# Attention scores from two float32r products per tile, made on chip, with a merged front

## Chip, core and metric

The kernel runs on one core of one Trainium2 chip. The time is the device time of one execution in microseconds, from the first instruction to the last, with a little around it. Three runs of the kernel before gave 888.09, 890.4 and 890.46 us; their median is 890.4 us.

## What is computed

One decoder layer with post-normalisation, for 4 sequences of 512 tokens with 256 features, all in float32. Only the first line is touched by the change:

```python
x = _layernorm(x + _L0_attn_ref(x, w_q, w_k, w_v, w_o))
#   q, k, v = x @ w_q.T, x @ w_k.T, x @ w_v.T            16 heads of 16
#   weights = softmax(einsum('bqhd,bkhd->bhqk', q, k) * 16**-0.5)
#   out     = einsum('bhqk,bkhd->bqhd', weights, v);  out @ w_o.T
x = _layernorm(x + _L0_xattn_ref(x, ctx, ctx, ...))      # 64 keys per sequence
x = _layernorm(x + _L0_ffn_ref(x, router_w, w1, w2))     # 8 experts, the best 2 per token
```

The scores go through an exponential, so they are needed nearly as exactly as float32 gives them.

## The kernel before

**Work and names.** There are NB = 4 sequences (batches) b. A *unit* u is four heads of one sequence (HG = 4 heads, NU = 4 units a batch, 16 units in all). A *tile* is 128 x 512 scores of one head; a unit has 16 tiles of scores with queries on the partitions, of which only the row maximum is wanted (*maximum tiles*, `max_half`, L1233), and 16 tiles with keys on the partitions, whose exponentials are kept (*exponential tiles*, `exp_tile`, L1288). The value product (`pv`, L1297) multiplies four exponential tiles, one of each head, with the values; its four heads lie on four groups of 32 columns of TensorE (PE), and a column of ones gives the sum of the softmax. The maximum of a query is subtracted inside the product of the exponential tile, as extra rows of the contraction.

**Exactness.** A score tile is one bfloat16 product. q and k are each split into three bfloat16 parts, and six products of parts (`Q_PART`, `K_PART`) are laid under each other as 96 rows of contraction; three rows more carry the parts of the maximum. To have these rows on the right partitions, the parts go to DRAM and come back.

**The front.** For each batch PE projects q, k and v in float32 (`project`, L1254, L1257), ScalarE (ACT) and VectorE (DVE) make the three parts (L732, L878, L735, L363), and the queue of SyncE (SP) writes them to DRAM (L387) and reads them back as stacks `qst` and `kst` in 12 DMAs (L393), `make_stacks`. The parts of batch b + 1 can't be overwritten before those of b are stored. Maximum tiles of the first two units run between the projections of batches 2 and 3. The three rows of maxima of unit 0 are written to `qst` by DMAs (`max_rows`, L400) that stand on SP's queue between the stacks.

**The units.** PE's order in `unit` (L1304) is written by hand: exponential tiles of unit u alternate with maximum tiles of unit u + 2, value products stand two tiles behind the fourth exponential tile, and the maxima of unit u + 1 are turned from partitions to rows once (`max_turn`, L1240). DVE takes the row maxima (`row_max`, L890), copies the turned maxima (`max_T`, L898) and the finished output of a unit to `oT` (L955). ACT takes the exponentials (L745). GpSimd (POOL) splits the maxima (`max_parts`) and lays out the values (`v_unit`). Four banks of PSUM hold maximum tiles, three hold exponential tiles, one the value products.

**Behind it.** From L1356 on, output projection, cross-attention, router and experts follow. The change leaves their code as it is, but for places in memory. Late weights and the residual x are loaded in the last batch of units.

The unit loop of PE, where its order is made:

```python
            for kt in range(QT):
                for h in range(HG):
                    exp_tile(u, HG * kt + h)
                    ...
                    if has_m and h < HALVES[kt]:
                        max_half(u + 2, half_at, j + 2)
                        half_at += 1
                    if h == 2 and kt > 0:
                        pv(u, b, kt - 1, j)
```

## Time and profile before

| | us |
|---|---|
| median of three runs | 890.4 |
| the profiled execution, as timed | 889.74 |
| its span (first to last instruction) | 888.0 |
| front: projections, stacks, holes, until the units run without a stop | 0 to 141.06 |
| the rest of the units of self-attention | 141.06 to 324.39 |
| everything behind | 324.39 to 888.0 |

The page gives the busy time of each engine over the whole span. Its 40 slices show where an engine is busy; a slice is 22.2 us. Since the stages have different limits, the busy time is read stage by stage (windows), and what an engine waits for is read from the chain of waits and from the instructions in order of time. A matmul's duration in the trace contains its latency; what it costs in a stream is the time from its start to the next start.

### The profile page before, as it was taken

The page shows a single profiled execution, that of the slowest core. Times are in us where ns is not written, and L with a number is a line of the kernel's source. Part 1 is how long each engine was busy: PE and PEld are TensorE (multiplying, and loading weights), DVE is VectorE, ACT ScalarE, POOL GpSimd, SP SyncE. Part 2 cuts the span into 40 slices and gives each one's busy share as a digit, 9 for nine tenths or more (in the row PEclk, how much of TensorE's full clock was granted, in tenths as well). Part 3 has the DMA queues.
Part 4 walks back from the last instruction along what each step waited for, and adds up shares of the span by engine and source line. Part 5 has one row for each costly group of instructions (what it writes and reads, how often), then busy time and mean ns, then how long its engine had stood idle before and what let it go on. Part 6 is the DMA issues. An engine that isn't in the chain of part 4 may idle for free.

```text
span 888.0 us, 13256 instructions
## 1 busy us (share of the span) xinstructions
PE 686.3 (77%) x4099; PEld 449.1 (51%) x4100; DVE 349.9 (39%) x750; ACT 285.8 (32%) x501; POOL 212.3 (24%) x265
## 2 busy tenths in 40 slices
PE   7572266999999986764677862099999999999980
PEld 3230111322222245541213652089999999999970
DVE  2252344888888546653443875000000000000004
ACT  3220133767666643332354211011111111111112
POOL 1020100111111122112111067213333333333322
PEclk9876786999999999886689995599999999999995
DMA  6999992000001430858713722356666566656615
GB/s 207 129 170 169 141 151 32 3 1 1 1 1 44 136 53 37 134 82 130 98 53 101 250 77 50 105 161 180 175 169 177 167 173 180 174 174 175 170 45 189
DMA packets 75777, 103.61 MB, mean 117 GB/s; under 512 B 15044, under 2 KB 60637, under 8 KB 75742
## 3 DMA queue, kind: packets, MB, share of 16 engines
q1 hardware_dynamic: 63006, 90.53, 45.0%
q0 software_dynamic: 8512, 8.44, 5.8%
q10 hardware_dynamic: 4224, 4.19, 1.7%
q8 instruction: 19, 0.31, 0.2%
q14 instruction: 16, 0.13, 0.1%
HBM read 82.95 MB, written 21.40 MB: 118 GB/s over the span
## 4 chain that ended last, share of the span: by engine, by line
PE 64%; DMA 14%; DVE 7%; SPq 5%; POOL 4%; issue 3%; ACT 2%; DVEq 0%; ACTq 0%; POOLq 0%
PE ps L1566 16%; PE ps L1577 15%; PE ps L1288 7%; DMA scrq<-parts 7%; PE ps L1297 7%; PE ps L1233 5%; SPq L393 3%; POOL metas L664 3%; DMA qst<-mT 3%; PE ps L1381 2%; PE ps L1454 2%; PE ps L1447 2%; DMA qst<-scr_q 1%; PE ps L1413 1%; DVE xr L993 1%
## 5 line engine op out<-in xcount | busy, mean ns | idle before, releaser
L890 DVE TENSOR_REDUCE nmx<-ps 128x1 f32<-128x512 f32 x256 | 160.4, 681 | 55.0 <-PE ps L1233 55.0
L745 ACT ACTIVATE probs<-ps 128x512 f32<-128x512 f32 x256 | 133.8, 606 | 93.7 <-PE ps L1288 93.6
L1566 PEld LDWEIGHTS ps<-xtT,w1c 128*128 128x128 f32 x1248 | 147.1, 194 | 4.3 <-issue 2.4
L1566 PE MATMUL ps<-xtT,w1c 128*128 128x128 f32 x1248 | 147.6, 277 | 1.8 <-ACT xtT L845 1.8
L1577 PE MATMUL ps<-wexp,hidT 128*128 x624 | 141.0, 379 | 0.0
L1198 DVE TENSOR_SCALAR yw<-ps,mt 128x256 f32<-128x256 f32 x39 | 18.9, 484 | 292.2 <-PE ps L1577 292.2
L1577 PEld LDWEIGHTS ps<-wexp,hidT 128*128 128x128 f32 x624 | 115.6, 190 | 14.2
L1288 PE MATMUL ps<-qst,kst 99*128 (+1 forms) x256 | 96.4, 396 | 33.9 <-DMA qst<-mT 31.8
L1233 PE MATMUL ps<-kst,qst 96*128 (+1 forms) x256 | 94.6, 396 | 33.6 <-DVE nmx L890 17.3
L851 ACT ACTIVATE hidT<-ps 128x1024 f32<-128x1024 f32 x39 | 40.0, 1024 | 229.8 <-PE ps L1566 229.8
L703 POOL DMA_INDIRECT acc<-yw,mt x39 | 61.7, 1582 | 172.0 <-DVE yw L1198 172.0
L1288 PEld LDWEIGHTS ps<-qst,kst 99*128 (+1 forms) x256 | 23.8, 99 | 120.3 <-issue 92.0
L1297 PE MATMUL ps<-probs,vu 128*32 128x512 f32 x512 | 68.2, 605 | 1.9 <-ACT probs L745 1.4
L1233 PEld LDWEIGHTS ps<-kst,qst 96*128 (+1 forms) x256 | 25.5, 100 | 66.0 <-issue 26.9
L808 ACT ACTIVATE probs<-ps 64x512 f32<-64x512 f32 x64 | 35.5, 587 | 42.9 <-PE ps L1447 42.8
L695 POOL DMA_INDIRECT xt<-x2d,mt x39 | 40.8, 1047 | 31.6 <-DMA mt<-metas 12.2
L532 POOL TENSOR_TENSOR m<-nmx,one 128x16 bf16<-128x16 f32 x16 | 3.5, 217 | 181.4 <-PE ps L1233 111.3
L1447 PE MATMUL ps<-qst,k2st 99*64 99x512 bf16 x64 | 27.1, 471 | 15.2 <-DMA qst<-mT 9.6
L664 POOL DMA_INDIRECT metas<-meta,slot x32 | 31.7, 990 | 22.4 <-DVE slot L1140 13.3
L1555 PE MATMUL ps<-identf,xt 128*128 128x128 f32 x78 | 15.2, 277 | 28.2 <-DMA xt<-x2d,mt 28.2
L878 DVE SCALAR_TENSOR_TENSOR tmp<-ps,parts 128x1024 f32<-128x1024 f32 x8 | 9.8, 1219 | 57.4 <-ACT parts L732 57.4
L1393 PE MATMUL ps<-identf,xr 128*128 128x128 f32 x64 | 14.1, 362 | 22.7 <-DVE xr L993 21.9
(162 smaller groups left out, 668.1 us busy)
## 6 DMA issues: line engine op xcount, KB each, us to landing
w1c<-in_w1T SPq DMA_DIRECT2D x39, 1024.0 KB
wexp<-in_w2T SPq DMA_DIRECT2D x8, 1024.0 KB, 5.5
qst<-scrq SPq DMA_DIRECT2D x24, 256.0 KB, 9.2
kst<-scrk SPq DMA_DIRECT2D x24, 256.0 KB, 19.7
qst<-scr_q SPq DMA_DIRECT2D x24, 256.0 KB, 8.8
scrq<-parts SPq DMA_DIRECT2D x4, 768.0 KB, 18.1
scrk<-parts SPq DMA_DIRECT2D x4, 768.0 KB, 18.6
scr_q<-parts SPq DMA_DIRECT2D x4, 768.0 KB, 3.4
```

What stands on the lines that cost most here:

```text
L664: pool.indirect_dma_start(metas, bass.IndirectOffsetOnAxis(slot[b % 2][:, k * QT + t:k * QT + t + 1], 0), meta[k][:, 2 * (QT * b + t):2 * ...
L695: pool.indirect_dma_start(xt[t % 2][:, :], None, x2d, bass.IndirectOffsetOnAxis(slot_meta(t, 0).bitcast(U32), 0), **checked()).then_inc(s_ ...
L703: pool.indirect_dma_start(acc, bass.IndirectOffsetOnAxis(slot_meta(t, 0).bitcast(U32), 0), yw[t % 2][:, :], None, **checked(), compute_op= ...
L745: act.activation(probs[n % 8][:, :], ps[:, 4 + n % 3, :], ACT.Exp).then_inc(s_exp, 1)
L851: act.activation(hidT[j % 2][:, :], bank(2 * (j % 2), 2), ACT.Gelu).then_inc(s_h, 1)
L890: dve.tensor_reduce(nmx[j % 2][:, k:k + 1], ps[:, slot, :], AX.X, ALU.max, negate=True).then_inc(s_mfree, 1)
L1233: pe.matmul(ps[:, tile_slot(j, k, isinstance(w, int) and w == 0), :], qst[0:ROWS, ds((w * HG + h) * S + qt * P, P)], kst[0:ROWS, ds((w * H ...
L1288: pe.matmul(ps[:, 4 + n % 3, :], kst[:, ds((u * HG + h) * S + kt * P, P)], qst[:, ds((u * HG + h) * S, S)], start=True, stop=True).then_in ...
L1297: mm = pe.matmul(ps[VW * h:VW * (h + 1), 7, :], vu[j % 2][:, (kt * HG + h) * VW:(kt * HG + h + 1) * VW], probs[(kt % 2) * HG + h][:, :], s ...
L1447: pe.matmul(ps[0:SC, 4 + h % 2, :], k2st[0:MROWS, ds((h * NB + b) * SC, SC)], qst[0:MROWS, ds((b * H + h) * S, S)], start=True, stop=True) ...
L1566: mm = pe.matmul(ps[:, 2 * (j % 2) + f // 4, f % 4 * P:(f % 4 + 1) * P], w1c[j % 2][:, k * FF + f * P:k * FF + (f + 1) * P], xtT[j % 2][:, ...
L1577: mm = pe.matmul(ps[:, 4 + j % 2, 0:D], hidT[j % 2][:, f * P:(f + 1) * P], wexp[:, ds(e * EW + f * D, D)], start=(f == 0), stop=(f == KF - 1))
```

## The change

**Scores.** The stacks, the three bfloat16 parts and the way through DRAM are gone. The weights of q and k are laid out with every head's 16 columns twice (`wqd`, `wkd`, by DVE for the first unit and POOL for the others), so that a projection of one unit (four heads) has 128 rows, 32 for each head, with q (or k) in them twice. From the projection in PSUM, ACT and DVE write four tiles of type float32r, a float32 of fewer mantissa bits: `qb` holds the high numbers of q, `qa` high and low numbers (the low ones negated), `ka` the high numbers of k, the second 16 rows with the sign turned, `kb` the low numbers of k, over whose second rows ones are laid. A score tile is then two products that add in one bank, each on the 32 rows of its head: `qa` with `ka`, and the first 16 rows of `qb` with `kb`. For exponential tiles the second product has two rows more, high and low number of the maximum against ones (`MAX_ROWS`). The four heads of a unit lie on four groups of 32 rows.

**Maxima.** They are turned as float32 without a split, DVE writes high and low numbers (`mT_hi`, `mT_lo`), and eight DMAs a unit put them in `qb`. Two DMAs a unit write the ones.

**Order.** A short front projects q0 and k0 of the first batch; 26 maximum tiles (`LEAD`) are taken ahead, with five more projections between. Then PE takes two exponential tiles, two maximum tiles, a value product after every second such step, and a projection of the same or the next batch at places of a table. Everything is unrolled. Maximum and exponential tiles have three banks each.

```diff
+LEAD = 26
+TURN_AT = 3
+HIGHS = 2 * HD
+MAX_ROWS = 2
+PROJECTIONS = ("q0", "k0", "q1", "k1", "v0", "q2", "k2", "v1", "q3", "k3")
...
+    PROLOGUE = {1: "q1", 4: "k1", 8: "v0", 12: "q2", 16: "k2"}
+    FIRST_BATCH_AT = {2: "v1", 6: "q3", 11: "k3"}
+    NEXT_BATCH_AT = [dict(zip(at, PROJECTIONS)) for at in
+                     ((15, 20, 25, 30, 35, 41, 46, 51, 57, 62), (3, 9, 17, 23, 29, 35, 41, 47, 53, 59))]
...
     @block.sync
-        def make_stacks(b):
...
+        def ones_rows(u):
+            sp.wait_ge(s_kb, u + 1)
+            for r in range(HD, HD + MAX_ROWS):
+                sp.dma_start(kb[u % (2 * NU)][r:P:HIGHS, :].bitcast(F32).rearrange("p (a t) -> p a t", a=HG),
+                             onesr[:, :].unsqueeze(1).to_broadcast([HG, HG, S // HG])).then_inc(s_one[u % NU], 16)
+        def max_rows(w):
+            sp.wait_ge(s_mfree, turn_slot(w) + 1)
+            for r, m in ((HD, mT_hi), (HD + 1, mT_lo)):
+                for i in range(HG):
+                    sp.dma_start(qb[w % (2 * NU)][HIGHS * i + r:HIGHS * i + r + 1, :].bitcast(F32).rearrange("p (a t) -> p a t", t=P),
+                                 m[w % 2][QT * i:QT * (i + 1), :].bitcast(F32)).then_inc(s_mrow[w % 2], 16)
...
     @block.scalar
+        def q_high(b, u, name):
+            act.wait_ge(s_proj, proj_number(b, name) + 1)
+            act.activation(qb[(NU * b + u) % (2 * NU)][:, :], ps[:, proj_bank(b, name), :], ACT.Copy).then_inc(s_qb, 1)
+        def k_high(b, u, name):
+            act.wait_ge(s_proj, proj_number(b, name) + 1)
+            act.activation(ka[(NU * b + u) % (2 * NU)][:, :], ps[:, proj_bank(b, name), :], ACT.Identity,
+                           scale=sign[:, 0:1]).then_inc(s_ka, 1)
...
+        for e in range(UNITS * TILES):
+            act.wait_ge(s_e, e + 1)
+            if e % HG == 0 and e >= 8:
+                act.wait_ge(s_pv, e // HG - 1)
+            act.activation(probs[e % 8][:, :], ps[:, 3 + e % 3, :], ACT.Exp).then_inc(s_exp, 1)
+            for b, name in projections_at(e):
+                evict(b, name)
...
     @block.vector
+        def q_both(b, u, name):
+            dve.wait_ge(s_qb, n + 1)
+            dve.scalar_tensor_tensor(out=qa[n % (2 * NU)][:, :], in0=ps[:, proj_bank(b, name), :], scalar=not_low[:, 0:1],
+                                     in1=qb[n % (2 * NU)][:, :], op0=ALU.mult, op1=ALU.add).then_inc(s_qa, 1)
+        def k_low(b, u, name):
+            dve.wait_ge(s_ka, n + 1)
+            dve.tensor_tensor(kb[n % (2 * NU)][:, :], ps[:, proj_bank(b, name), :], ka[n % (2 * NU)][:, :],
+                              ALU.subtract).then_inc(s_kb, 1)
...
+        for e in range(UNITS * TILES):
+            maxima(e + LEAD)
+            if e % TILES == 1 and e >= TILES:
+                o_out(e // TILES - 1)
+            for b, name in projections_at(e):
+                evict(b, name)
...
     @block.tensor
+        def max_tile(w, k):
...
+            pe.matmul(ps[:, n % 3, :], qa[u][both, qt * P:(qt + 1) * P], ka[u][both, :], start=True, stop=False)
+            pe.matmul(ps[:, n % 3, :], qb[u][highs, qt * P:(qt + 1) * P], kb[u][highs, :], start=False,
+                      stop=True).then_inc(s_mready, 1)
...
+        def exp_tile(e):
+            if e >= 3:
+                pe.wait_ge(s_exp, e - 2)
+            w, both, more = u % (2 * NU), slice(HIGHS * i, HIGHS * (i + 1)), slice(HIGHS * i, HIGHS * i + HD + MAX_ROWS)
+            pe.matmul(ps[:, 3 + e % 3, :], ka[w][both, kt * P:(kt + 1) * P], qa[w][both, :], start=True, stop=False)
+            pe.matmul(ps[:, 3 + e % 3, :], kb[w][more, kt * P:(kt + 1) * P], qb[w][more, :], start=False,
+                      stop=True).then_inc(s_e, 1)
...
+        for e in range(0, UNITS * TILES, 2):
+            for pair in range(2):
+                exp_tile(e + pair)
+            for pair in range(2):
+                maxima(e + LEAD + pair)
+            if e % HG == 0 and e >= HG:
+                pv(e // HG - 1)
+            for b, name in projections_at(e) + projections_at(e + 1):
+                project(b, name)
```

The order on PE, in the middle of a unit. Before (L1297 is the value product, L1288 an exponential tile, L1233 a maximum tile, L1240 the turn):

```order
L1297 MATMUL ps<-probs0_113,vu0_121 32x512 [waits probs_ready,v_unit_ready]
L1297 MATMUL ps<-probs1_114,vu0_121 32x512
L1297 MATMUL ps<-probs2_115,vu0_121 32x512
L1297 MATMUL ps<-probs3_116,vu0_121 32x512
...
L1288 ISA [waits probs_ready]
L1288 MATMUL ps<-qst_98,kst_99 128x512
...
L1233 ISA [waits max_scores_used]
L1233 MATMUL ps<-kst_99,qst_98 128x512
```

And after, in unit 6 of the changed kernel (L1292 and L1293 are the two products of an exponential tile, L1241 and L1242 those of a maximum tile, L1273 a projection, L1306 the value product):

```order
L1293 MATMUL ps<-qb6_116,kb6_132 128x512
L1241 MATMUL ps<-ka7_125,qa7_109 128x512 [waits max_scores_used]
L1242 MATMUL ps<-kb7_133,qb7_117 128x512
L1241 MATMUL ps<-ka7_125,qa7_109 128x512 [waits max_scores_used]
L1242 MATMUL ps<-kb7_133,qb7_117 128x512
L1273 MATMUL ps<-xTb2_139,wqd_153 128x512 [waits v_half_ready]
L1273 MATMUL ps<-xTb2_139,wqd_153 128x512
L1292 MATMUL ps<-qa6_108,ka6_124 128x512 [waits probs_ready]
L1293 MATMUL ps<-qb6_116,kb6_132 128x512
L1292 MATMUL ps<-qa6_108,ka6_124 128x512 [waits probs_ready]
...
L1306 MATMUL ps<-probs0_142,vu1_135 32x512 [waits probs_ready,o_ready]
```

Each tile has two products in a row where it had one, tiles go in pairs, and the projections of later batches stand between them.

The order on SP's queue at the start. Before, the maxima of unit 0 (L400) stand behind the stacks (L387, L393) of three batches:

```order
L387 DMA scrq<-parts_101 128x2x1536 [waits part3_ready]
L387 DMA scrk<-parts_102 128x2x1536 [waits part3_ready]
L393 DMA qst<-scrq 16x16x512 [waits q_parts_stored,stacks_loaded]
L393 DMA qst<-scrq 16x16x512 x5
L393 DMA kst<-scrk 16x16x512 [waits k_parts_stored]
L393 DMA kst<-scrk 16x16x512 x5
L400 DMA qst<-mT_96 1x16x128 [waits max_scores_used]
L400 DMA qst<-mT_96 1x16x128 x2
```

After (L433 are the ones, L440 the maxima):

```order
L404 DMA wv_s<-in_wvT 128x2x256
L400 DMA xTb_138<-in_xT 128x2x512
L411 DMA metas<-pad_meta 128x258 [waits pad_ready]
L433 DMA kb_126<-onesr 4x4x128 [waits k_low_ready]
L433 DMA kb_126<-onesr 4x4x128
L433 DMA kb_127<-onesr 4x4x128 [waits k_low_ready]
L433 DMA kb_127<-onesr 4x4x128
L440 DMA qb_110<-mT_hi_93 1x4x128 [waits max_scores_used]
L440 DMA qb_110<-mT_hi_93 1x4x128 x3
L440 DMA qb_110<-mT_lo_95 1x4x128 x4
```

The 48 stack reads and 8 stores are gone from the queue; a unit has eight small DMAs for its maxima where it had three, and two for ones.

## Rows read from the trace of the kernel before

**Rows 1.** The page: engines' busy time, and PE's busy tenths in 40 slices
```profile
PE 686.3 (77%) x4099; PEld 449.1 (51%) x4100; DVE 349.9 (39%) x750; ACT 285.8 (32%) x501; POOL 212.3 (24%) x265
PE   7572266999999986764677862099999999999980
```

**Rows 2.** Windows: stretch, its length, then busy time of each engine, clock, DMA
```profile
core 0: us, PE busy (x) PEld busy (x) DVE busy (x) ACT busy (x) POOL busy (x), PEclk, DMA share, GB/s
238.06:250.04 11.98, 11.90 (x66) 3.50 (x66) 10.57 (x19) 8.29 (x16) 1.49 (x5) 1.00 0.01 1
...
0.00:141.06 141.06, 69.79 (x226) 33.18 (x228) 44.71 (x63) 30.71 (x37) 15.92 (x37) 0.78 1.03 157
141.06:324.39 183.33, 179.36 (x966) 53.00 (x966) 143.20 (x244) 124.99 (x240) 20.90 (x78) 0.98 0.09 27
324.39:888.00 563.61, 437.17 (x2907) 362.94 (x2907) 162.01 (x443) 130.15 (x224) 175.46 (x150) 0.88 0.54 136
```

**Rows 3.** The chain of waits: start us, us, what
```profile
31.48 20.09 DMA scrq<-parts
...
61.79 20.52 DMA scrq<-parts
...
95.94 16.09 DMA scrq<-parts
...
125.26 15.65 DMA qst<-mT
...
340.36 1.72 PE ps L1413 x4
```

**Rows 4.** Instructions in order of time, PE, in a unit: start us, us, engine, line
```profile
230.05 0.38 PE L1233 MATMUL ps<-kst,qst 96*128 x1
230.36 1.07 PE L1297 MATMUL ps<-probs,vu 128*32 128x512 f32 x8
231.36 0.39 PE L1288 MATMUL ps<-qst,kst 99*128 x1
231.59 0.38 PE L1233 MATMUL ps<-kst,qst 96*128 x1
231.81 0.38 PE L1288 MATMUL ps<-qst,kst 99*128 x1
```

**Rows 5.** Instructions in order of time, where self-attention ends
```profile
324.39 0.69 DVE L955 COPY oT<-ps 128x512 f32<-128x512 f32 x1 [5.29 <-PE ps L1297]
```

**Rows 6.** Instructions in order of time, PE, projections of the first and second batch
```profile
5.78 5.85 PE L1254 MATMUL ps<-xTb,wq_s 128*128 128x512 f32 x8 [5.78 <-DMA xTb<-in_xT]
...
14.90 3.62 PE L1257 MATMUL ps<-wv_s,xTb 128*128 128x256 f32 x16
...
18.36 3.60 PE L1254 MATMUL ps<-xTb,wq_s 128*128 128x512 f32 x8
```

**Rows 7.** Instructions in order of time, DVE and ACT, runs of one operation without a stop
```profile
228.08 3.67 DVE L890 TENSOR_REDUCE nmx<-ps 128x1 f32<-128x512 f32 x6
```
```profile
227.62 3.54 ACT L745 ACTIVATE probs<-ps 128x512 f32<-128x512 f32 x7 [1.56 <-PE ps L1288]
```

**Rows 8.** Groups by line: out<-in, shapes, count | busy us, mean ns | idle before
```profile
L878 DVE SCALAR_TENSOR_TENSOR tmp<-ps,parts 128x1024 f32<-128x1024 f32 x8 | 9.8, 1219 | 57.4 <-ACT parts L732 57.4
...
L898 DVE COPY mT<-ps 48x128 bf16<-48x128 bf16 x16 | 3.3, 207 | 3.4 <-PE ps L1240 3.4
```

**Rows 9.** DMAs of the maxima: issue, time to landing, and one line's instructions (ns min/median/max)
```profile
303.12 1.82 SPq L400 DMA_DIRECT2D qst<-mT  x3
```
```profile
qst<-mT SPq DMA_DIRECT2D x48, 4.0 KB, 1.7
```
```profile
L1288 PE MATMUL ps<-qst,kst x256: 376/380/634, 110.9 to 322.2; 99*128 x96, 99*128 99x512 bf16 x32
```

**Rows 10.** Instructions in order of time, PE, behind the hole of 15.8 us
```profile
141.46 0.63 PE L1233 MATMUL ps<-kst,qst 96*128 x1
141.89 0.63 PE L1288 MATMUL ps<-qst,kst 99*128 x1
```

567 lines of the change are left out of this document (252 added, 315 removed).

## Prediction

> **What bounds the kernel now.** First the page [rows 1]: PE is busiest, with uneven digits in the first six slices and nines in the next eight, so there are stages to be told apart. The windows give them [rows 2]: self-attention has a front of 141.06 us in which PE is busy 69.79, then 183.33 us in which PE is busy 179.36; what follows takes 563.61 us. The chain of waits shows what the front waits for [rows 3]: DMAs that carry the bfloat16 parts to DRAM (20.09, 20.52 and 16.09 us) and a 15.65 us landing of the maxima behind them. The reader is to see two stages with different limits: transfers, then PE. A unit of the second stage takes 11.98 us (PE 11.90, DVE 10.57, ACT 8.29) [rows 2]. PE's sum for it: 32 score tiles at 0.22 from start to start, 6.9-7.0, and four value products at 1.00 plus 0.09 around each, 4.4; turning and waits make up 0.6 [rows 4].
>
> The change touches self-attention alone. Its end stands in the trace as the last copy of oT, 324.39 + 0.69 = 325.1 us [rows 5]. The code behind it computes the same with the same instructions, and its loads come earlier, so I keep its time as it is, though an earlier load could save some or a changed memory place cost some: neither has a row, and I give both together 2 us either way. The profiled execution took 889.74 us in all; forecasts are 889.7 plus the shift of the 325.1, and that execution lies 0.7 below the median of the runs.
>
> **Removed.** The four rounds through DRAM, the 12 stack DMAs of a batch and the four waits of [rows 3], 72.4 us on the chain, all go. So does the split on POOL.
>
> **New front, to the first exponential.** Weights and x arrive about as before, PE started at 5.78 [rows 6]. The doubling of the first columns on DVE is short (128 columns); I take 0.5. A projection of one unit is two float32 products of 512 columns, four instructions. Eight such took 5.85 in the first, half-clocked call and 3.60 later [rows 6], so q0 costs up to 3.4, k0 1.7. Both evictions (ACT, then DVE) end at 14. For a DVE reduction I read (3.67 - 0.68)/5 = 0.60 between starts, for an exponential (3.54 - 0.60)/6 = 0.49 [rows 7]. The 26 tiles ahead are bound by DVE: 15.6. Four evictions among them cost DVE 0.6 each, 2.4 (1219 ns for twice the columns [rows 8]), and since DVE stands still behind each until PE has projected and ACT has copied, 1.5 more each, 5.9 in all: 37.9 us. The maxima then wait for eight DMAs issued one by one at 1.82/3 = 0.6, and 1.7 to land [rows 9]: 6.5 from DVE's copy at 35.3. So the first exponential's scores start near 42, where before they started at 110.9 [rows 9], with the hole of [rows 3] to 141.06.
>
> **PE's work from there.** I count in the order of the instructions and cost by rows:
> - 230 maximum tiles and 256 exponential tiles. Each is now two float32r products of 512 columns in one group of 32 rows, the second adding to the bank of the first. *Rate*: no row shows float32r. From below, a bfloat16 product of 512 columns is 0.22 [rows 4]; from above, a float32 product of 512 columns is two instructions of 0.43 (1.72 for four [rows 3]). Float32 thus spends four times 0.215, which I read as high and low of either side, four pairs; a float32r product is one such pair, so I take 0.217. *Overlap*: no row shows row groups. Column groups do overlap: eight instructions of 0.43 on four groups take 1.07 [rows 4]. Here the second product of a tile must follow the first on the same rows, and the next tile stands behind it in order; so I take that only neighbours overlap, one product's time per tile. 486 x 0.217 = 105.5.
> - 64 value products. Before: 1.09 each. When PE leaves a run of row groups, the last product (0.21) has no neighbour. 64 x 1.30 = 83.
> - 33 projections. Before, q and k cost 7.2 a batch; the doubled columns make it eight of 1.72 [rows 3], 13.8. Of q and k 26 are left, each with 0.2 of change of tiling (the margins around a value product) and 0.21 of run-out: 26 x 2.13 = 55.4. Seven of v (3.62 for 16 instructions, so 1.81 a half [rows 6]) at 2.2: 15.5.
> - Turns of maxima 15 x 0.5 = 7.5 (0.1 of work, the rest changes of tiling and run-out); the two context products are 24 instructions like those of v, 5.4, with 0.8 of changes: 6.2.
>
> Sum 273, or 17.9 a unit while projections last (6.9 + 5.2 + 5.3 + 0.5), 12.6 for the last four. DVE's sum is 256 x 0.60 + 16 x 0.6 + 32 x 0.6 + 16 x 0.42 = 189 (two mT copies of 0.21 for one [rows 8]), ACT's 256 x 0.49 + 40 x 0.5 = 145: neither is the bound, and their longer evictions hide beside PE. PE's own waits I got by stepping the orders of PE, ACT and DVE with these durations, where a tile starts once the one three before it has been read from its bank (a result is readable 0.44 after its product's start, an estimate from the 0.38 of a product in [rows 4] and 0.06, and a freed bank is seen 0.06 after the reading ends): 0.9 a unit for eleven units (DVE or ACT behind a projection), 9.7 in the last four, where the 6.5 of the maxima's DMAs exceeds the eight tiles it has (2 x 1.85) and the last unit runs at ACT's pace. Together 20. End: 42.4 + 273 + 20 + 0.9 for the last copy = 336. Against 325.1 that is 11 later. **Forecast 901 us**: the front gains 99 us, and a unit that took 12.0 takes 18.
>
> The Trainium skill, TensorE: Matmul & The Clock Gate, Part 3, says that matmuls start and end in program order; by that rule the overlap is between neighbours, as taken above, and the trace's groups of eight (start order unknown) do not contradict it. The Trainium skill, TensorEngine Tiling (Array Packing), Key Properties, says that a change of tiling mode drains the engine; the trace's margin for it is the 0.1 on either side of a value product, and the sum would be the same by the one and the other.
>
> **Rivals.**
> 1. *All four groups run at once* (other side: faster). Column groups show it: two instructions per group and still 1.07 for eight [rows 4]. If the first products of four tiles start together and their second ones after them, a tile costs 0.11, saving 52; the run-out before each of some 110 changes grows from 0.21 to 0.43, and DVE's and ACT's latencies are no longer hidden, so PE's waits grow. Stepped through: 313, or 12 before 325.1: 878 us (870 to 885 for changes of tiling at 0.05 to 0.1). It decides from 0.19 us a tile downwards. Against it: the two products of a tile stand in order. The Trainium skill, TensorE: Matmul & The Clock Gate, Part 3, has a measured 3.07 times for four row groups, which would carry a good part of this rival; no row here shows row groups.
> 2. *No overlap*: every product 0.217 alone, a tile 0.43. 486 x 0.21 = 102 more, less 24 of run-outs and some 21 of waits: 393, 958 us.
> 3. *Two columns' time per column* for the 4-byte operand, as one float32 instruction has (0.43). With neighbours overlapping, 443: 1007 us; with all groups at once, 359: 923 us.
> 4. *The clock stays at 1.2 GHz* because few rows are at work. After the 15.8 us hole a tile took 0.43 instead of 0.22 [rows 10], and the second stage had a granted clock of 0.98 [rows 2]. Against it: value products and gapless work held it. PE's work would double: above 1100 us.
> 5. *It doesn't shorten the front*: excluded by construction, since no tile waits for DRAM; a front of 60 instead of 42 would add 18, 919 us.
>
> **How the numbers follow.** Chances: forecast (neighbours overlap, 890 to 920, with changes of tiling from 0.05 to 0.15, tiles to 0.23, front 38 to 50) 0.46; rival 1 0.27; rival 2 0.10; rival 3 0.09; rival 4 0.02; a still better course, where PE's changes of tiling cost nothing and DVE's 189 bounds, near 42 + 189 x 1.1 = 250-300, so under 866, 0.06. Range 866 to 960, which leaves out about 0.17. A measurement of this kernel tells 0.3% (2.7 us) from no change: faster 0.38 (rival 1, the better course, and 0.05 of the forecast's lower edge), same 0.08 (from the forecast's lower edge), slower 0.54.
>
> **What would show it.** Start-to-start of the score products on PE: 0.217 for each second one confirms the rate, and a neighbour's start within 0.01 of a second product the overlap; four starts within 0.03 would be rival 1; 0.43 rival 3. The first product for exponentials near 42 us. Units 18 us apart for the first eleven and 12.6 to 15 for the last four. DVE idle about a third of the stage, waiting for PE. No DMA share to speak of after 60 us. The forecast is wrong above all if the cost per tile is not 0.22: each 0.01 moves the end by 4.9 us.

## The result, and the profile after

The change makes the kernel slower: **939.7 us** (median of four, 935.1 to 941.1) against 890.4; ratio 1.054, 95% interval 1.049 to 1.059. The forecast was 901, so the direction was right and the size was not: 11 us forecast, 49 measured. The profiled execution took 935.1. Executions of one kernel differ here by up to 4%, the longer ones with a lower mean clock (e11 has 899.2 us at 0.896 and 934.7 at 0.863), so the medians below leave out executions more than 1.5% above the fastest of their kernel, and a profile shows one execution, for e1, e13 and e18 one of the longer ones.

The page of the changed kernel, PE's busy time and the 40 slices of PE and of its granted clock (a slice is 23.3 us):

```profile
PE 776.9 (83%) x4691; PEld 501.0 (54%) x4692; DVE 373.0 (40%) x794; ACT 291.4 (31%) x521; POOL 185.6 (20%) x184
...
PE   5889999999999988676577786139999999999990
...
PEclk9879999999997558978669996559999999999995
```

Set against [rows 1]: the uneven front is gone, and nines run through self-attention. But eleven of them stand in a row where before there were seven, and the clock has 7, 5 and 5 tenths near the end of the stage. The windows by stage, which answer to [rows 2] (stretch, length, busy time of each engine, clock, DMA share, GB/s):

```profile
0.00:49.07 49.07, 31.82 (x86) 13.55 (x88) 27.64 (x42) 5.74 (x8) 10.41 (x34) 0.87 0.13 41
49.07:285.65 236.58, 226.24 (x1348) 91.42 (x1352) 150.97 (x255) 122.37 (x227) 0.00 (x0) 0.96 0.07 19
285.65:367.14 81.49, 75.49 (x354) 29.31 (x354) 32.64 (x56) 33.35 (x62) 0.65 (x2) 0.62 0.06 20
367.14:933.40 566.26, 443.38 (x2907) 366.76 (x2907) 161.75 (x443) 129.99 (x224) 174.57 (x149) 0.87 0.54 136
196.24:213.30 17.06, 16.45 (x110) 6.45 (x106) 12.36 (x23) 9.72 (x18) 0.00 (x0) 1.00 0.06 19
```

Front, twelve units with projections, the last four units, everything behind, and one unit by itself at full clock. Self-attention ends with the last copy of oT, the row that answers to [rows 5]:

```profile
366.46 0.69 DVE L949 COPY oT<-ps 128x512 f32<-128x512 f32 x1 [1.35 <-PE ps L1306]
```

It ends 42 us later than before (325.1); what stands behind it takes 566.3 where it took 562.9. (In the experiments below, which leave that part alone, it takes 560.1 to 570.0.) The forecast's end was 336. Its 31 us are spread so:

| stretch | forecast | measured |
|---|---|---|
| to the first exponential | 42.4 | 49.07 |
| twelve units with projections | 225.6 | 236.6 |
| last four units, context, last copy | 68 | 81.5 |

**How PE's time is made up.** PE, DVE and ACT in order of time, in one turn (two tiles for exponentials and two for maxima, with what follows them) that has a projection, at full clock (start us, us, engine, line, operation; in brackets the idle time ahead and who ended it). L1292 and L1293 are the first and the second product of a tile for exponentials, L1241 and L1242 those of a tile for maxima, L1273 a projection, L1306 a value product:

```profile
205.54 0.50 PE L1292 MATMUL ps<-qa,ka 32*128 32x512 f32 x2
205.56 0.19 PEld L1241 LDWEIGHTS ps<-ka,qa 32*128 32x128 f32 x2
205.56 0.50 PE L1241 MATMUL ps<-ka,qa 32*128 32x512 f32 x2
...
205.89 0.40 PE L1293 MATMUL ps<-qb,kb 18*128 18x512 f32 x2
205.90 0.40 PE L1242 MATMUL ps<-kb,qb 16*128 16x512 f32 x2
...
206.22 1.98 PE L1273 MATMUL ps<-xTb,wkd 128*128 128x512 f32 x4
206.32 1.08 ACT L739 ACTIVATE probs<-ps 128x512 f32<-128x512 f32 x2 [2.35 <-PE ps L1293]
206.40 1.29 DVE L868 TENSOR_REDUCE nmx<-ps 128x1 f32<-128x512 f32 x2 [0.88 <-PE ps L1242]
...
208.14 0.50 PE L1292 MATMUL ps<-qa,ka 32*128 32x512 f32 x2
...
208.82 1.07 PE L1306 MATMUL ps<-probs,vu 128*32 128x512 f32 x8
...
208.97 0.69 DVE L899 TENSOR_TENSOR kb<-ps,ka 128x512 fp32r<-128x512 f32 x1 [1.27 <-ACT ka L715]
209.57 3.77 DVE L868 TENSOR_REDUCE nmx<-ps 128x1 f32<-128x512 f32 x6
209.81 0.50 PE L1292 MATMUL ps<-qa,ka 32*128 32x512 f32 x2
...
210.31 0.18 PEld L1241 LDWEIGHTS ps<-ka,qa 32*128 32x128 f32 x1 [0.19 <-DVE nmx L868]
```

Three things are to be seen. First, the first products of all four tiles start within 0.02 us, and the four second ones 0.34 later, though the program has each tile's second product right behind its first: four tiles cost 0.68 (205.54 to 206.22), 0.17 each. Second, from 205.54 to 209.81 PE has not one gap (0.68 + 1.92 + 0.68 + 0.99), while ACT has stood 2.35 and DVE 0.88 and 1.27. Third, right behind it DVE has six maxima in a row to catch up, and PE waits for banks (210.31). Units last 17.1 to 23.1 us behind the first one, and where the wanting engine changes within a unit, busy shares don't add up.

### The profile page after: what moved, and what is told of

It reads as the page before. It is cut to its first block, busy times and chain, and to the rows that moved or that the text cites. A ratio compares the mean times of both kernels' runs of the same rounds, so it can differ in the third digit from the quotient of the medians.

```text
span 933.4 us, 13012 instructions
## 1 busy us (share of the span) xinstructions
PE 776.9 (83%) x4691; PEld 501.0 (54%) x4692; DVE 373.0 (40%) x794; ACT 291.4 (31%) x521; POOL 185.6 (20%) x184
## 3 DMA queue, kind: packets, MB, share of 16 engines
q10 hardware_dynamic: 4496, 4.72, 1.8%
## 4 chain that ended last, share of the span: by engine, by line
PE 71%; DVE 9%; DMA 6%; ACT 4%; POOL 3%; issue 3%; SPq 3%; DVEq 0%; POOLq 0%; ACTq 0%
PE ps L1563 15%; PE ps L1574 14%; PE ps L1306 7%; PE ps L1273 7%; PE ps L1292 6%; PE ps L1293 3%; POOL metas L643 3%; PE ps L1378 3%; ACT probs L739 2%; PE ps L1241 2%; PE ps L1451 2%; PE ps L1444 2%; SPq L440 2%; PE ps L1280 1%; DVE nmx L868 1%
## 5 line engine op out<-in xcount | busy, mean ns | idle before, releaser
L1241 PE MATMUL ps<-ka,qa 32*128 32x512 f32 x256 | 93.2, 549 | 8.0 <-DVE nmx L868 6.2
L1292 PE MATMUL ps<-qa,ka 32*128 32x512 f32 x256 | 88.6, 541 | 11.7 <-ACT probs L739 8.4
L682 POOL DMA_INDIRECT acc<-yw,mt x39 | 61.7, 1582 | 172.1 <-DVE yw L1204 172.1
L1292 PEld LDWEIGHTS ps<-qa,ka 32*128 32x128 f32 x256 | 34.9, 204 | 109.5 <-ACT probs L739 55.4
L1306 PE MATMUL ps<-probs,vu 128*32 128x512 f32 x512 | 80.2, 700 | 3.3 <-ACT probs L739 3.3
L1242 PE MATMUL ps<-kb,qb 16*128 16x512 f32 x256 | 75.5, 434 | 0.0
L607 POOL MEMSET probs<- 64x512 f32 x8 | 3.8, 519 | 352.9 <-PE ps L1306 352.9
L1293 PE MATMUL ps<-qb,kb 18*128 18x512 f32 x256 | 73.5, 439 | 0.0
L1241 PEld LDWEIGHTS ps<-ka,qa 32*128 32x128 f32 x256 | 36.7, 200 | 26.2 <-DVE nmx L868 15.7
L799 ACT ACTIVATE probs<-ps 64x512 f32<-64x512 f32 x64 | 35.4, 587 | 42.9 <-PE ps L1444 42.8
L1273 PE MATMUL ps<-xTb,wqd 128*128 128x512 f32 x64 | 34.6, 667 | 6.3 <-DVE wqd L910 6.3
L1273 PE MATMUL ps<-xTb,wkd 128*128 128x512 f32 x64 | 36.9, 705 | 2.4 <-DVE wkd L910 2.4
```

The costliest lines, as they stand in the source:

```text
L682: pool.indirect_dma_start(acc, bass.IndirectOffsetOnAxis(slot_meta(t, 0).bitcast(U32), 0), yw[t % 2][:, :], None, **checked(), compute_op= ...
L1241: pe.matmul(ps[:, n % 3, :], qa[u][both, qt * P:(qt + 1) * P], ka[u][both, :], start=True, stop=False)
L1242: pe.matmul(ps[:, n % 3, :], qb[u][highs, qt * P:(qt + 1) * P], kb[u][highs, :], start=False, stop=True).then_inc(s_mready, 1)
L1273: mm = pe.matmul(ps[:, at, :], wd[:, (k * NU + i) * P:(k * NU + i + 1) * P], xTb[b][:, k * S:(k + 1) * S], start=(k == 0), stop=(k == KD - 1))
L1292: pe.matmul(ps[:, 3 + e % 3, :], ka[w][both, kt * P:(kt + 1) * P], qa[w][both, :], start=True, stop=False)
L1293: pe.matmul(ps[:, 3 + e % 3, :], kb[w][more, kt * P:(kt + 1) * P], qb[w][more, :], start=False, stop=True).then_inc(s_e, 1)
```

## The experiments

Every kernel is the changed one with an edit. The range is that of all executions, the ratio has its 95% interval. The last three columns are of the profiled execution: the start of the first exponential's scores, the twelve units with projections (from there to the twelfth copy of oT), and the last four (to the sixteenth copy), each with its mean granted clock in brackets (1.00 is 2.4 GHz, 0.50 is 1.2 GHz).

| kernel | median us (range) | ratio to before | first | twelve units | last four |
|---|---|---|---|---|---|
| changed | 939.7 (935.1-941.1) | 1.049-1.059 | 49.1 | 236.6 (0.96) | 80.8 (0.62) |
| e1_fill_bf16 | 923.3 (916.2-934.7) | 1.028-1.042 | 56.5 | 245.3 (0.92) | 64.8 (0.97) |
| e10_front_fill | 942.0 (936.8-945.1) | 1.048-1.057 | 57.5 | 237.1 (0.96) | 80.8 (0.62) |
| e13_spread | 943.5 (934.5-952.9) | 1.052-1.066 | 45.5 | 261.4 (0.89) | 75.2 (0.82) |
| e17_lead28 | 957.9 (952.6-977.0) | 1.077-1.098 | 49.1 | 258.9 (0.93) | 78.5 (0.70) |
| e18_lead30 | 925.5 (922.8-941.2) | 1.026-1.046 | 52.7 | 243.8 (0.92) | 79.1 (0.63) |
| e4_front | 934.1 (930.5-938.3) | 1.043-1.057 | 42.8 | 240.8 (0.93) | 80.8 (0.62) |
| e8_hole | 939.0 (933.6-943.3) | 1.048-1.064 | 63.3 | 237.6 (0.92) | 75.1 (0.70) |
| e5_half_proj | 902.7 (900.5-921.3) | none | 47.9 | 223.9 (0.89) | 69.3 (0.80) |
| e7_split | 921.6 (915.6-934.8) | 1.025-1.042 | 51.8 | 236.0 (0.95) | 68.9 (0.83) |
| e2_alternate | 928.1 (921.1-935.8) | 1.031-1.050 | 48.8 | 244.4 (0.92) | 66.8 (0.85) |
| e3_one_product | 920.3 (918.2-923.0) | 1.027-1.038 | 44.3 | 238.8 (0.87) | 67.4 (0.67) |
| e14_max_prod | 917.7 (917.4-932.7) | 1.027-1.037 | 46.8 | 235.7 (0.92) | 68.8 (0.80) |
| e11_max_one | 908.2 (899.2-934.7) | 1.017-1.026 | 44.0 | 224.9 (0.97) | 63.6 (0.87) |
| e9_all | 909.2 (906.4-911.6) | 1.018-1.030 | 49.1 | 229.0 (0.93) | 62.6 (1.00) |
| e12_best | 909.7 (901.1-913.9) | 1.010-1.020 | 54.7 | 212.9 (0.99) | 78.7 (0.72) |
| e15_one_fill | 912.0 (902.0-928.9) | 1.016-1.029 | 40.6 | 240.6 (0.89) | 65.5 (1.00) |
| e16_one_spread | 924.0 (917.5-945.9) | 1.031-1.043 | 40.5 | 252.4 (0.87) | 69.3 (0.93) |
| e19_one_front_fill | 905.4 (902.5-923.5) | 1.002-1.022 | 40.5 | 237.2 (0.92) | 61.7 (1.00) |

The clock differs from kernel to kernel, so a median mixes what an edit does to the work with what happened to the clock. The traces tell them apart. Count the units from 0 and take one from one copy of oT to the next: at a clock of 1.00 the same unit lasts the same to within 0.06 us in the changed kernel, e1, e4, e8 and e10 (unit 11 takes 17.05 to 17.06 in all five). So any other kernel's units at 1.00 can be set against them, one by one:

| kernel | units 2 to 11 that can be compared | mean difference, us a unit |
|---|---|---|
| e18_lead30 | 6 | +0.16 |
| e17_lead28 | 7 | +1.35 |
| e2_alternate | 5 | -0.20 |
| e7_split | 6 | -0.12 |
| e5_half_proj | 5 | -1.49 |
| e14_max_prod | 6 | -0.70 |
| e11_max_one | 9 | -0.74 |
| e3_one_product | 1 | -1.68 |

### Do four row groups run at once?

The forecast took it that only neighbours overlap. With `LEAD` = 26 the two tiles for exponentials and the two for maxima of a turn lie on four row groups (26 leaves 2 by 4); with 28 on two; 30 is the control.

```diff
-LEAD = 26
+LEAD = 28
```

> The changed kernel with the maxima 28 tiles ahead of the exponentials where it was 26: the same work, but the two tiles for exponentials and the two for maxima of a turn now lie on the same two row groups. If four row groups at once are what makes a group of four cost 0.68: four products then follow each other on each row group, 0.34 + 3 x 0.22 = 1.0, and 128 such groups cost 0.32 more each, 41 us, where PE is the bound; part of it falls into waits: 960 to 980 from 939.7. Rival (program order decides and neighbours overlap alone, as forecast): 0.217 a tile in either order, only 1.2 us for two more tiles in the front: 938 to 943.

> The changed kernel with the maxima 30 tiles ahead, the control of the run with 28: four row groups in a turn as with 26, and four tiles more in the front (4 x 0.60 = 2.4 us later). If the row groups decide, 938 to 943, like 26. If a longer lead by itself matters (the maxima's DMAs have four more tiles of time at each unit's start): up to 5 us less.

Measured: 957.9 with 28, near the 960 to 980 that row groups would make, and 925.5 with 30. PE in order of time in e17, in a turn of the same kind:

```profile
194.64 0.50 PE L1292 MATMUL ps<-qa,ka 32*128 32x512 f32 x2
194.97 0.40 PE L1293 MATMUL ps<-qb,kb 18*128 18x512 f32 x2
195.21 0.40 PE L1241 MATMUL ps<-ka,qa 32*128 32x512 f32 x2
195.44 0.41 PE L1242 MATMUL ps<-kb,qb 16*128 16x512 f32 x2
195.78 1.99 PE L1280 MATMUL ps<-wv_s,xTb 128*128 128x256 f32 x8
```

The maxima's products start behind the second products of the exponentials, on whose rows they are, and a group of four takes 1.14 where it took 0.68. Unit 11 at full clock, in the changed kernel, e17 and e18 (stretch, length, busy times, clock):

```profile
268.59:285.65 17.06, 16.32 (x110) 6.26 (x106) 12.35 (x22) 9.72 (x18) 0.00 (x0) 1.00 0.11 34
289.47:307.99 18.52, 18.12 (x109) 7.58 (x109) 12.44 (x22) 9.73 (x18) 0.00 (x0) 1.00 0.09 31
279.31:296.49 17.18, 16.66 (x110) 6.32 (x106) 12.37 (x22) 9.63 (x18) 0.00 (x0) 1.00 0.10 34
```

So the row groups decide and not the order of the program: what the forecast called rival 1 is how the chip works here, and e17 is nearer to the machine that the forecast had in mind. The control missed its range (938 to 943) by 12 us on the faster side. Its units at full clock are no shorter than those of the changed kernel (+0.16), so the longer lead doesn't save work; what made e18 faster than the changed kernel was not found. The Trainium skill, TensorE: Matmul & The Clock Gate, Part 3, has products of distinct row groups run concurrently (this trace agrees: 0.02 us between four starts) and all of them start in program order; here, the first products of three tiles start 0.33 us ahead of a second product that stands before them in the program, so the measurement decides against that half.

### What does the clock take?

After the last projection nothing but score tiles and value products is left. e1 adds one product of no use on all 128 rows every two tiles in the last four units:

```diff
+            if e >= 192 and e % 2 == 0:
+                pe.matmul(bank 6, identb, onesb broadcast to 512 columns)
```

> The changed kernel, and in the last four units of self-attention (no projections left) PE also takes one bfloat16 product of the identity with a row of ones on all 128 rows every two tiles, 32 in all, into a bank that nobody reads. Theory A, the clock: from 292 to 353 us of the changed kernel the granted clock was 0.50 while only products on 32 rows and value products were left; the last four units took 80.8 us where the hand count had 60. If these fillers keep the clock at 2.4 GHz, that loses 10 to 20 us against 939.7: 920 to 930 us, and the windows after 290 us show a clock near 1.0. Rival: the pace of these units is that of the handing over between PE, ACT and DVE and not of PE's clock; then the clock comes back and the time stays within 3 us, or the fillers' own 32 x (0.22 + changes of tiling of 0.1 to 0.3) add 10 to 16 us: 940 to 955. Third: the clock falls in spite of them, 945 to 955.

Unit 13 of the changed kernel, and then the last four units of the changed kernel and of e1:

```profile
303.95:325.85 21.90, 21.90 (x102) 8.63 (x102) 11.56 (x19) 8.69 (x16) 0.00 (x0) 0.50 0.08 26
285.65:366.46 80.81, 75.49 (x354) 29.31 (x354) 31.96 (x55) 33.35 (x62) 0.00 (x0) 0.62 0.05 17
301.72:366.56 64.84, 61.68 (x386) 23.89 (x385) 31.67 (x55) 32.73 (x62) 0.00 (x0) 0.97 0.07 23
```

At a clock of 0.50, that is 1.2 GHz, unit 13 is PE work without a gap; the same unit of e1 takes 15.10 at 1.00. e1's last four units take 64.8 us, where the changed kernel needs 80.8, and the median is 16.4 lower in spite of 32 more products. So theory A holds; the fillers cost PE 0.32 each, so the fall itself costs somewhat more than the 16 us that come back. (The execution of e1 that was profiled ends self-attention at 367.3, like the changed kernel: its front and its first twelve units were at a lower clock, 7.4 and 8.7 us longer.) And the fall did not come from idling: in the six us before 291.8 PE never stood for more than 0.21 us. A value product costs 1.94 there:

```profile
296.85 1.94 PE L1306 MATMUL ps<-probs,vu 128*32 128x512 f32 x8
```

What makes the clock fall is not shown. It is not the lack of products on all 128 rows alone: e2, e7, e11 and e14 have no fillers and no projections there either, and their units 12 and 13 run at 0.98 to 1.00. Nor do fillers always hold it: with the same 32 fillers as e1, e12 stands at 0.50 for 44 of its last 79 us. In e13 the projections are spread to the tile at which each is needed.

> The changed kernel with the projections of the last three batches spread up to the tile at which each is needed (the last one at tile 209 of 256 instead of 187), the same work in all. Theory D (turns with a projection are PE's alone, turns without one are waits for banks) and theory A (without projections the clock falls) both expect a gain: fewer projections in the crowded units, and the clock up for another 20 tiles: 5 to 12 us less, 928 to 935 from 939.7. Rival, theory C (only PE's sum counts and it is the same) with the clock falling after the last projection just as long: within 3 us.

Measured 943.5, with executions on both sides of the changed kernel's: no gain, where 5 to 12 us were expected. In its profile the last four units gained 5.6 us and the first twelve lost 24.8, with a clock of 0.89 where the changed kernel has 0.96; the clock record has fourteen stretches at 0.50 up to the end of self-attention, where the changed kernel has eight, of the same length together (96 us). A projection at half clock holds up everybody, as ACT in e13:

```profile
208.35 0.60 ACT L725 ACTIVATE vu<-ps 128x512 f32<-128x512 f32 x1 [5.34 <-PE ps L1281]
```

In the front the clock brought nothing either:

> The changed kernel with products that nobody reads ahead of the first exponential: eight of identity by identity (bfloat16, 512 columns, 128 rows) before the first projection, and two behind each of the 26 tiles for maxima. In the changed kernel's front three stretches of 3.4, 3.4 and 14 us had a granted clock of 0.50, in other runs 20 to 34 us; k0 took 3.49 there and k2 3.66 where 1.92 is the full price. Theory A in the front: with the clock up, k0, k2 and the evictions behind them come 3 to 6 us earlier, 934 to 937 from 939.7; it would also be nearer 925 if the half clock in the front is what spreads the runs (935 to 941). Rival: DVE (26 x 0.60) bounds the front, so that PE's clock there counts nothing, and 52 products more add up to 52 x 0.22 + changes of tiling: 940 to 952.

942.0: the clock up to 50 us rose from 0.86 to 0.97, but the first exponential came at 57.5 where it came at 49.1. The time is inside the rival's range, and the rival's second half is what the trace shows: the added products are on the path. DVE waits 10.5 us for the maxima's products there, against 2.5 in the changed kernel, so in e10 it is PE and not DVE that bounds the front.

### The front

```diff
         pool.wait_ge(s_w[n], 16)
+        if n == 0:
+            pool.wait_ge(s_wd0, 2 * KD)
```

> The changed kernel, where POOL waits for DVE's four doublings of the first unit's columns before it doubles the others. In the changed kernel DVE's two doublings of wk took 2.79 us each beside POOL's work, and the first projection of k started at 12.37 instead of near 8.5. If POOL's work beside it makes them slow: each back to 0.5 or less, k's projection 3 to 5 us earlier, the first exponential at 45 instead of 49.07, and 935 us. Rival: DVE is slow there by itself, or POOL's later start makes the second unit's columns late; then within 2 us of 939.7, or up to 5 slower.

The doubling of wk on DVE in the changed kernel, beside POOL's own doublings, and in e4, where POOL waits:

```profile
6.81 5.51 DVE L910 TENSOR_SCALAR wkd<-wk_s 128x128 f32<-128x128 f32 x2
```
```profile
6.40 0.36 DVE L912 TENSOR_SCALAR wkd<-wk_s 128x128 f32<-128x128 f32 x2 [0.38 <-DMA wk_s<-in_wkT]
```

The two doublings took 0.86 and 4.72 us (2.79 is their mean) and became 0.22 each, and the first exponential starts at 42.8 where it started at 49.07. The median is 934.1, 5.6 less; the two ranges overlap. The Trainium skill, SBUF — State Buffer, Terms, says that DVE and GpSimd arbitrate for one pair of ports and that the loser is blocked for a whole instruction; the trace agrees in that DVE's second doubling took some twenty times its time and ended at 12.32, behind POOL's two long MEMSETs (8.32 to 11.86 us).

> The changed kernel with the last three projections of the first batch (v1, q3, k3) ahead of the first exponential, in banks 6, 5 and 7, where PE stands while the DMAs of the first maxima are under way (40.6 to 49.07, nothing but DVE's and SP's work in it). Theory C and D alike: three projections of 1.92 and two changes of tiling each go from the units into a hole that is there anyway, 6 to 8 us less: near 933, with the first exponential still at 49. Rival: PE has these projections beside waits of the readers in the units anyway: within 2 us. Against it: if the evictions behind the last one end after 49, each us is lost.

939.0: nothing. PE in order of time in e8, from v1 to the first exponential:

```profile
54.05 3.78 PE L1282 MATMUL ps<-wv_s,xTb 128*128 128x256 f32 x8
57.63 2.38 PE L1275 MATMUL ps<-xTb,wqd 128*128 128x512 f32 x4
59.84 1.88 PE L1275 MATMUL ps<-xTb,wkd 128*128 128x512 f32 x4
63.27 0.50 PE L1294 MATMUL ps<-qa,ka 32*128 32x512 f32 x2 [1.55 <-issue]
```

The hole was not where I had put it. The ten tiles for maxima behind the turn come first, so the three projections start when the DMAs are nearly done, the first at half clock, and the first exponential slips from 49.07 to 63.27. From there to the end of self-attention e8 takes 313.4 us where the changed kernel takes 318.1. So the front lost 14.2 and the units gained 4.7, and self-attention ends 9.5 later. In the profiled executions 6.1 of these don't show in the total, since what stands behind, the same code, took 560.1 us in e8 and 566.2 in the changed kernel.

### What does a projection cost, and what the handing over?

e5 leaves out half of each projection of q and k, e7 cuts each in two halves two tiles apart, with its evictions later.

> The changed kernel, and each projection of q and k takes only the first half of its contraction (left out: the second float32 product, half of the sum over the model's width), 25 such products less behind the first exponential. In the changed kernel's trace a turn with a projection is PE work without a gap (0.68 + 1.92 + 0.68 + 1.00 = 4.27 from 205.54 to 209.81) while DVE waits up to 1.27 and ACT 2.35 for tiles; a turn without one has PE waiting for them. Theory C (projections on PE's path at their full price): 25 x 0.96 = 24 us less, near 915, from 939.7. Rival (banks and readers set the pace, PE catches up): less than 6 us. Theory A may hide some of it, if the lower clock begins earlier with less work.

> The changed kernel with each projection behind the first exponential in two halves, the second one two tiles later, and its evictions by ACT and DVE two tiles later too. PE's products are the same and the changes of tiling are 28 more. Theory D (a projection in one piece of 1.92 lets ACT and DVE run dry, since three banks hold 1.5 to 1.8 us of work, and in the turns without one PE waits for them; the two wants add up instead of lying side by side): the halves of 0.96 fall into waits of about 1 us; 12 units x 2 us = 24 less, less 28 x 0.2 of changes = 5: near 920. Rival, theory C (what counts is PE's sum): 28 changes of tiling more, 940 to 947.

e5: 902.7 (its executions lie 20 us apart), 37 less where theory C said 24. At full clock its units are 1.49 shorter, where the halves of two projections are 1.92: a projection's time on PE is on the path at about three quarters of its price. Another part of the gain is clock: 11.5 us lie in the last four units, in which there is no projection, at 0.80 instead of 0.62.

e7: 921.6, 18.1 less with the same work and more changes of tiling, which looks like theory D. But the last four units of the changed kernel, e7, e2, e14 and e12 tell where such gains lie:

```profile
285.65:366.46 80.81, 75.49 (x354) 29.31 (x354) 31.96 (x55) 33.35 (x62) 0.00 (x0) 0.62 0.05 17
287.73:356.63 68.90, 59.71 (x354) 23.25 (x354) 31.43 (x54) 32.80 (x62) 0.00 (x0) 0.83 0.07 20
293.21:359.96 66.75, 57.20 (x354) 22.55 (x354) 30.81 (x55) 33.02 (x62) 0.00 (x0) 0.85 0.06 20
282.54:351.35 68.81, 57.04 (x318) 21.09 (x312) 31.36 (x56) 32.92 (x62) 0.00 (x0) 0.80 0.06 20
267.58:346.27 78.69, 76.59 (x350) 26.61 (x349) 30.41 (x51) 33.30 (x62) 0.00 (x0) 0.72 0.06 18
```

e7's twelve units, where all its halves lie, take 236.0 against 236.6; its last four, where it has the very products of the changed kernel, take 11.9 us less at a higher clock. At full clock its units are 0.12 shorter in the mean (the halves move work between neighbours, so single ones differ by -1.3 to +0.8; units 6 to 9 together are 1.7 shorter), where theory D asked for 2 in each. So theory D is refuted as an account of this gain, and why the clock held longer is not shown.

> The changed kernel with one tile for exponentials and one for maxima in turn, where it took two and then two. Theory B, the handing over: in a unit PE has 14.7 us of work by the durations in the changed kernel's trace, but a unit takes 17 to 23; PE stands because ACT gets two tiles together and then none, and DVE likewise. In turn each gets a tile every 0.5 us: 1 to 2 us less a unit, 915 to 925 us. Rival: PE's products start in four row groups at once whatever the order, the banks (three for each) decide, and the time stays within 4 us of 939.7. Against the change of order: a value product or a projection that stands between may split the groups of four more often, +5 to +10.

928.1, 11.6 less, and the same picture: 0.20 a unit at full clock, where theory B said 1 to 2, and 14 us in the last four units at 0.85 of the clock. Feeding the readers in turn is worth some 3 us by itself, an estimate from 0.20 in each of 16 units.

> The changed kernel with only the first product of each score tile, on two row groups' worth of parts as before; left out is the second product (low times high, and the maxima that are subtracted), and the exponential is scaled by a quarter instead, so that it stays finite. PE has 486 products less. Theory B (a tile's way from its first product to the reader, 0.34 longer by the second product, is in the circle PE to reader to bank to PE): a circle is gone through once for two tiles, so 16 x 0.34 = 5.4 us a unit go, 16 units 87 us: 850 to 870 us, and units of 12 to 14 us. Theory C (PE's own work alone): a quad of four tiles goes from 0.68 to 0.34, 486/4 x 0.34 = 41 us: near 899. Theory A speaks too: with less work the granted clock may be 0.5 for longer, in which case the last units gain nothing (905 to 925).

920.3, only 19.4 less, though all 512 second products were gone. Theories B and C had it lower; theory A's range, 905 to 925, holds it. The windows from 50 to 350 us, changed kernel and e3:

```profile
50.00:350.00 300.00, 286.01 (x1618) 113.54 (x1615) 178.53 (x301) 149.32 (x277) 0.00 (x0) 0.87 0.06 18
```
```profile
50.00:350.00 300.00, 265.56 (x1198) 89.95 (x1196) 178.57 (x305) 150.48 (x286) 0.00 (x0) 0.83 0.06 17
```

A quarter of the instructions is gone, PE is still "busy" 265 of 300 us, and the clock is lower, 0.83. The one unit of e3 that can be compared is 1.68 shorter at full clock, which for twelve units would be 20 us; yet they took 238.8, 2 more than in the changed kernel, with 62 us at half clock in them where it has 21. With less to do PE ran more slowly. To take the parts apart, e14 drops the second product of the maxima alone, e11 the second row of maxima and its four DMAs a unit as well.

> The changed kernel with one product for each maximum, but with both rows of maxima and all DMAs as they were. e11, which had one row too, gave 28.4 us. Theory B (DVE's tile comes 0.34 earlier and PE's group is lighter): all but a few of these, 911 to 917. Theory E (the turn, DVE's subtraction and the four further DMAs at each unit's start are what e11 saved): only 5 to 10 us, 930 to 935.

> The changed kernel with one product for each maximum (the second one left out; the value subtracted is then only near the maximum and the same in numerator and sum, so the result stays) and with one row of maxima instead of high and low: 256 products, 15 subtractions on DVE and 64 DMAs less. Theory C (PE's sum): a group of four takes 0.68 because two products follow each other, and those for exponentials still do, so PE's sum stays nearly the same: within 4 us of 939.7. Theory B (way to the reader): DVE gets its tile 0.34 earlier: 16 x 8 x 0.2 = 20 us less at most, 920. Theory E (the maxima's DMAs at each unit's start): four fewer DMAs of 0.6 in a row, up to 2.4 us less where a unit waits for them; the trace has only 1.9 us of such waits from 100 to 280, and 2.5 before the first exponential: 935.

917.7 and 908.2. By the medians the maxima's second products alone are worth as much as all second products in e3 (22 us). By the units at full clock they are worth 0.70 each, 11 us in all sixteen by estimate; the rest lies in the last four units, where e14 has 27 us at half clock and the changed kernel 61. So theory B was right in kind and at most half in size. That the 0.70 is the way to DVE and not PE's lighter group is argued, not shown: a group of four still takes 0.67 in e14. The second row and its DMAs bring nothing in the units with projections (e11 has 0.74 there), but 1.2 us in each of units 12 and 13 (14.3 in e14, 13.1 in e11) and 2.8 ahead of the first exponential: theory E holds where a unit is short. e11 computes the same result as before, since whatever is subtracted cancels between numerator and sum. The waits of the changed kernel and of e11 (engine, line, waited for; us, times, longest):

```profile
ACT probs L739 <- PE ps L1293: 99.6, 64, 10.0
PEld ps L1292 <- ACT probs L739: 55.4, 75, 1.4
...
DVE nmx L868 <- PE ps L1242: 48.8, 42, 3.5
```
```profile
PEld ps L1288 <- ACT probs L739: 77.3, 92, 1.4
ACT probs L739 <- PE ps L1289: 75.1, 55, 7.2
...
DVE nmx L868 <- PE ps L1239: 28.6, 32, 3.3
```

DVE's waits fall by 20 and ACT's by 24, while PE's for ACT rise by 22: part of each gain turns into the next wait.

### Do the gains add up?

> The changed kernel with five edits together: projections in halves, three of them in the hole before the first exponential, one tile of each kind in turn, POOL's doubling behind DVE's, and the bfloat16 fillers in the last four units. One by one the three that have run gave 15.5 (fillers), 10.2 (in turn) and 5.6 us (front); by theory D the halves give 15 to 20 more and the hole 7. If they add: 939.7 - 15.5 - 10.2 - 5.6 - 18 - 7 = 883, faster than the kernel before (890). Rival: turning and halving lessen the same waits, so that one of the two is worth nothing: 893 to 900. Clock: if PE's fuller time keeps it up anyway, the fillers are worth less than alone.

> All edits together: halves, three projections in the hole, tiles in turn, POOL's doubling later, fillers in the last four units, in the first 14 tiles and in the front, and one product and one row for maxima. The combination without the last three gave 909.2 with a first unit at half clock for 17 us (8 lost) and 30 us of half clock in the front. If the fillers keep the clock there, 8 to 10 less; one row of maxima lets the first exponential begin 2.5 earlier, and DVE waits less: 895 to 900. For below 890 the units with projections, 18.3 us on average where PE's own sum is 15, would have to fall to 16.5. Rival: the units' time is PE's sum with its changes of tiling, and fillers only add: 905 to 912.

> e11 (one product and one row for maxima, 911.3) with tiles in turn, POOL's doubling behind DVE's, and two bfloat16 fillers every two tiles in the last four units. Units 13 and 14 of e11 took 13.1 us at full clock, the last two 16.9 and 20.5 with 17 us of half clock. If the causes add: 5.6 for the front, 5 to 10 for the clock, 0 to 4 for the order: 892 to 900. Rival: twice the fillers' work (64 x 0.22 and changes of tiling, 20 us) eats what the clock gives: 905 to 915.

> e11 with tiles in turn, POOL's doubling behind DVE's, the projections spread up to tile 209 and single fillers every two tiles from tile 212. By theories A and D the spread projections hold the clock where e15 needs fillers, and lie in waits: 885 to 893, which would be level with or better than the kernel before (890 to 893). Rival: the last units fall to half clock in spite of it, 900 to 905.

> e11 (one product and one row for maxima, 911.3) with POOL's doubling behind DVE's and single bfloat16 fillers every two tiles in the last four units, in the changed kernel's own order. If these add to e11 as they did alone (5.6 and 15.5, the latter less here, since only 17 us of the last units had the lower clock): 894 to 902. Rival: the clock falls somewhere else instead, 905 to 912.

909.2, 909.7, 912.0, 924.0 and 905.4: in the medians they don't add. e11 alone has 908.2; halves, turns, front and fillers bring at most 3 us on top of it, and spreading (e16) comes out 12 above e15. No version beats the kernel before (890): the nearest, e19, has a ratio of 1.002 to 1.022.

The traces show why. The work does add where it can be compared: units 2 and 3 of e15, with tiles in turn and one product for maxima, are 1.0 shorter at full clock, where e2 is 0.25 and e11 0.75 shorter. What doesn't add is the clock. The last four units stand at 80.8 us with 61 of them at half clock, and fillers, turns, halves and one product for maxima each bring them to between 61 and 69: each was credited with the same 12 to 19 us, and that can be had once. Where the clock is up already a filler only costs: units 12 and 13 take 13.1 in e11 and 14.4 and 14.3 in e19. And a clock held up in one stretch can be low in another: e19 and e15 have 1.00 in the last four units and 0.92 and 0.89 in the first twelve, while e12 has 0.99 in the first twelve, which take 212.9 us, 23.7 less than in the changed kernel (three projections stand ahead of them), and 0.72 in the last four. How low the clocks of other executions were, stretch by stretch, no run shows.

## Why the prediction was wrong in size

**The step that failed is the clock.** The sum prices every product at 2.4 GHz, and the half clock stands beside it only as rival 4, at a chance of 0.02, "against it: value products and gapless work held it". The twelve units in the order of the changed kernel come to 227.5 us at full clock (22.8 for unit 0 in e10, 183.2 for units 2 to 11 in the five kernels, and 21.5 for unit 1, an estimate: 23.1 less what a stretch of 3.4 us at half clock takes from a unit, 1.6), and the last four to 64.8 (e1, with fillers). Forecast were 225.6 and 68. Measured are 236.6 and 80.8: 9 and 16 us are clock, 25 of the 34.5 that the profiled execution lies above the forecast. The rest is the front, 6.7, and what stands behind, 3.3.

- **Rate of float32r**: right. Where one row group's products follow each other they start every 0.23 to 0.24 (e17's rows), one pass; taken was 0.217.
- **Overlap, "only neighbours"**: wrong. Four tiles cost 0.68 and not 0.87 plus a run-out. PE's own work by measured durations: 486/4 x 0.68 + 64 x 0.99 + 33 x 1.92 + 6 for turns + 6 for the context = 221, where the forecast had 273. The 52 that rival 1 wanted to save were saved. e17 shows that it is the row groups that do it.
- **PE's waits, 20 in all**: wrong too, by as much the other way. Self-attention from the first exponential on has 318 us, of which 221 are work and 25 clock; 72 are waits. Rival 1 was stepped with some 50 and came to 313. The hand recurrence had the right order, but it let PE run ahead of readers that stand behind a projection; the trace has ACT and DVE dry in the turns with a projection and PE waiting in the others. That the sum of work and waits is right to 2 us at full clock (292.3 against 293.6) is luck: two errors of some 50 cancel.
- **Units**: 17.9 plus 0.9 forecast for the first twelve, 19.7 measured and 19.0 at full clock: near, but as the sum of two errors, PE's work 3.1 too high and its waits 3 too low.
- **Last four units**: 12.6 to 15 each forecast, 20.2 measured. At 0.97 of the clock (e1, with fillers) 16.2. Rival 4 had the half clock, but as a state of the whole stage ("above 1100"). It came for 61 us of it and cost 16. Its reason, "few rows are at work", is not borne out as it stands: the same tiles ran at full clock in units 12 and 13 of e2, e7, e11 and e14. "Gapless work held it" was taken from the kernel before, whose tiles filled 99 rows, and is refuted: the clock fell and stayed down in gapless work.
- **Front**: 42.4 forecast, 49.07 measured; "I take 0.5" for the doubling was the term. DVE's part took 5.51 beside POOL. With POOL out of the way it is 42.8 (e4), so the rest of that sum was right. Of the 6.3 us 5.6 show in the medians.
- **A projection**: 1.92 with its changes, 2.13 forecast. Right within a tenth.
- **Behind self-attention, ±2**: 3.3 more, a little outside; the same code took 560.1 to 570.0 in the other runs, so the ±2 was narrower than the differences between executions.
- **Rivals 2 and 3** (no overlap, two columns' time): both excluded by the same rows. **Rival 5**: the front was shortened, from 110.9 to 49.07 for the first exponential.
- DVE idle a third of the stage: busy 151 of 236.6, as said.

The median lies 4.6 above the profiled execution.

## What to carry to other kernels

Before crediting an edit with a gain, find a stretch that both kernels ran at the same granted clock and compare it there. Here such stretches repeat to within 0.06 us and show gains of 0.1 to 1.5 us a unit, while the last four units alone moved by up to 19 us, for the most part with the clock; several edits seemed to add up to a faster kernel because each had been credited with the same lost clock. Place instructions of few rows so that successive ones lie on different row groups; a lead of 28 instead of 26 cost 1.35 us in each unit of 17 to 19. Where a stage has one engine gapless in some turns and waiting in others, its time is not the sum of the busiest engine's work: price the turns one by one. After taking work from TensorE, read the granted clock again before the time: a quarter fewer instructions came with a lower clock.
